# A windowed attention rewritten as banded blocks on small TensorE tiles

## The reference

```python
# x normalised over its last axis; cond = ctx_4096; B = 32, C = 64, T = 512, 8 heads of 8 channels
q = Wq x + bq;  k = Wk cond + bk;  v = Wv cond + bv          # 64 x 64 weights over the 64 rows
k, v = pad by 8 on the left and 7 on the right along T
idx = arange(T)[:, None] + arange(16)[None, :]
dots = einsum('bhdt,bhdtw->bhtw', qh, k[:, :, idx]) * 8 ** -0.5
out = einsum('bhtw,bhdtw->bhdt', softmax(dots), v[:, :, idx])
x = x + tanh(g_xattn[0]) * (Wo out + bo)
```

## Time and profile before

| | |
|---|---|
| median of 3 runs | 1720.14 us (1711.69 to 1721.57) |
| the profiled execution, its own time | 1712.46 us |
| its span | 1710.6 us |
| TensorE / VectorE / GpSimd / ScalarE busy | 80% / 62% / 25% / 25% |
| instructions | 16,681 |
| the first attention in the span | 0 to 637 us |

### The profile page before, as it was taken

The page is one execution under the profiler, slowest core; times in us unless marked ns, Lnnn a source line. Parts: engine busy times, 40 slices in busy tenths (PEclk is TensorE's granted clock), DMA queues, the critical chain, the costliest instruction groups (busy, mean ns, idle before and its releaser), DMA issues. The chain is left out here.

```text
span 1710.6 us, 16681 instructions
## 1 busy us (share of the span) xinstructions
PE 1363.9 (80%) x4738; PEld 798.8 (47%) x4739; DVE 1059.5 (62%) x1664; ACT 421.5 (25%) x1173; POOL 435.7 (25%) x118
## 2 busy tenths in 40 slices
PE   4176578755058639899989998999899979899998
PEld 1032256422047516455545554555455534477753
DVE  3399999999999988235722672257325755522226
ACT  3011210000010023233422442244224422044430
POOL 1366189966069500000000000000000000033225
PEclk9588879978578869999999999999999999899999
DMA  6811140040000035110001000100000017155657
GB/s 221 240 51 72 62 98 0 0 147 0 0 0 0 0 119 202 51 25 1 1 0 25 0 0 0 25 0 0 0 0 0 0 74 319 55 161 166 169 167 253
DMA packets 61266, 115.83 MB, mean 68 GB/s; under 512 B 21280, under 2 KB 25760, under 8 KB 60320
## 3 DMA queue, kind: packets, MB, share of 16 engines
q1 hardware_dynamic: 49296, 82.23, 14.4%
q0 software_dynamic: 6400, 20.98, 4.6%
q10 hardware_dynamic: 5520, 12.06, 1.9%
HBM read 77.50 MB, written 37.75 MB: 67 GB/s over the span
## 5 line engine op out<-in xcount | busy, mean ns | idle before, releaser
L954 POOL DMA_INDIRECT w_sb<-xn_rows,tok_of x48 | 45.6, 949 | 1006.7 <-DVE tok_of L1308 913.7
L242 POOL TENSOR_TENSOR gprod<-dots,v_h 128x4096 f32<-128x4096 f32 x16 | 188.7, 11830 | 115.2 <-ACT dots L282 115.2
L233 POOL TENSOR_TENSOR gprod<-q_h,k_h 128x4096 f32<-128x4096 f32 x16 | 161.9, 10138 | 106.6 <-DMA k_h<-by_row 62.1
L699 PE MATMUL big_ps<-wo_sb,ot 128*128 128x512 f32 x384 | 176.2, 594 | 7.6 <-DVE ot L813 7.6
L318 PE MATMUL sum_ps<-gprod,ident 128*128 128x512 f32 x256 | 122.9, 637 | 70.8 <-POOL gprod L233 50.5
L690 PE MATMUL big_ps<-ht,wq_sb 128*128 128x512 f32 x384 | 171.4, 592 | 0.0
L332 PE MATMUL sum_ps<-gprod,ident 128*128 128x256 f32 x512 | 134.0, 427 | 40.1 <-POOL gprod L242 40.1
L656 ACT ACTIVATE probs<-s_ps,npeak 128x128 f32<-128x128 f32 x256 | 91.8, 363 | 269.8 <-PE p_ps L746 233.0
L332 PEld LDWEIGHTS sum_ps<-gprod,ident 128*128 128x128 f32 x512 | 110.3, 218 | 63.1 <-issue 43.3
L318 PEld LDWEIGHTS sum_ps<-gprod,ident 128*128 128x128 f32 x256 | 51.9, 206 | 141.6 <-issue 85.8
L398 DVE TENSOR_REDUCE o_h<-prod 128x256 f32<-128x4096 f32 x16 | 116.4, 7273 | 0.6
(11 more groups left out here) (193 smaller groups left out, 2170.0 us busy)
## 6 DMA issues: line engine op xcount, KB each, us to landing
wr<-in_w_routed SPq DMA_DIRECT2D x4, 3072.0 KB, 22.4
y_rows<-h_sb SPq DMA_DIRECT2D x48, 256.0 KB, 2.0
by_row<-stage ACTq DMA_DIRECT2D x8, 768.0 KB, 3.8
X<-in_x SPq DMA_DIRECT2D x4, 1024.0 KB, 9.0
cond<-in_ctx SPq DMA_DIRECT2D x16, 256.0 KB, 2.7
by_row<-stage ACTq DMA_DIRECT2D x8, 512.0 KB, 3.3
q_h<-by_row SPq DMA_DIRECT2D x4, 1024.0 KB, 8.6
k_h<-by_row SPq DMA_DIRECT2D x4, 1024.0 KB, 13.2
```

The source lines that it names most:

```text
L233: nc.gpsimd.tensor_tensor(gprod[:, s], q_h[:, :, :], k_h[:, :, bass.ds(4 * i + (2 * s + 1), DIM)], ALU.mult).then_inc(multiplied, 1)
L242: nc.gpsimd.tensor_tensor(by_window(gprod[:, s]), half_of(dots, half), window(d, half), ALU.mult).then_inc(multiplied, 1)
L699: last = nc.tensor.matmul(ps[:, :], ot[:, a % 2, c, k * P:(k + 1) * P], wo_sb[:, a * HC + c, :], start=(c == 0), stop=(c == HC - 1))
```

## The change

The first attention stays in the layout of rows (128 partitions are two batches of 8 heads of 8 channels) and on chip; `by_row` goes. A tile of 128 rows has four quarters of 32 partitions, each four heads (`HG`) of one batch. Positions are cut into blocks of 32 (`BLK`), and a block of queries meets a span of 47 keys (`SPAN`). Scores are dense 32 x 47 blocks; a table `band` adds -1e30 outside the window.

- GpSimd spreads the keys, and likewise the queries, into a block-diagonal form with one copy per head, zero elsewhere (`heads_apart`, L220): 128 x 4 x 512.
- Scores are computed twice. A "score" unit has queries on partitions; VectorE takes its maximum and subtracts it, ScalarE takes the exponential, VectorE sums (L509, L510, L501). Maximum and reciprocal sum (`stats`) are turned by TensorE into rows (L440). A "rescore" unit, one tile later, has the other layout, subtracts the maximum by 16 small matmuls (L401) and goes through ScalarE's exponential into `probs` (`weigh`). A unit covers a quarter and half the positions; there are 8 of each kind per tile, each in one PSUM bank out of six.
- Values: four zero products open the accumulation (L413), then four phases of 64 products on 32x32 tiles (L427), each phase waiting for the one before it. VectorE scales (L527), TensorE applies Wo (L445), ScalarE applies gate and bias, GpSimd adds to X (L231).
- All loops are unrolled in the program. VectorE's first statistics cover four tiles only before the work begins (`deviate`).

The diff, cut to its core (line numbers above are the new kernel's, from L111 on):

```diff
-        q_h = sb("q_h", [P, HD, DIM])
-        k_h = sb("k_h", [P, HD, TPAD])
...
+        q_bd, k_bd = sb("q_bd", [P, 2, HG, SPREAD]), sb("k_bd", [P, 2, HG, SPREAD])
+        v_bd = sb("v_bd", [P, 3, CH, 4, HG, BLK])
...
+        def units(i):
+            order = []
+            for half in range(2):
+                for sc in range(2):
+                    for g in range(2):
+                        first, second = (True, 0, g, sc), (False, 1, g, sc)
+                        if half:
+                            first, second = (False, 0, g, sc), (True, 1, g, sc)
+                        order += [u for u in (first, second) if (i < TILES if u[0] else i > 0)]
+            return order
...
+            def heads_apart(out, a):
+                return nc.gpsimd.tensor_tensor(out, a.unsqueeze(1).to_broadcast([P, HG, DIM]),
+                                               table["head"].unsqueeze(2).to_broadcast([P, HG, DIM]), ALU.mult)
...
+            for i in range(TILES + 1):
+                order = units(i)
...
+                for step in range(len(order) + 3):
+                    for r in range(4):
+                        if step < len(order):
...
+                            nc.tensor.matmul(ps[r * BLK:(r + 1) * BLK, 0:UNIT], ident[rows, rows], band[rows, :],
+                                             start=True, stop=False)
+                        for half in range(2):
+                            if 0 <= step - half - 1 < len(order):
...
+                                if u[0]:
+                                    last = nc.tensor.matmul(dst, q_sb[rows, i % 2, t:t + BLK], k_bd[rows, i % 2, :, t:t + SPAN],
+                                                            start=False, stop=bool(half))
...
+                                    nc.tensor.matmul(dst, k_sb[rows, (i - 1) % 3, t:t + BLK],
+                                                     q_bd[rows, (i - 1) % 2, :, t:t + SPAN], start=False, stop=False)
+                        if 0 <= step - 3 < len(order) and not order[step - 3][0]:
...
+                            for j in range(4):
...
+                                last = nc.tensor.matmul(dst, pick_peak[rows, r, :], window(stats_t[rows, (i - 1) % 2, t:], 2),
+                                                        start=False, stop=(r == 3))
...
+                    for phase in range(4):
+                        if phase:
+                            pe.wait_ge(phase_done, 4 * n + phase)
+                        for c in range(CH):
+                            for h in range(HG):
+                                for j in range(4):
+                                    q = (j + phase) % 4
...
+                                    last = nc.tensor.matmul(out_ps[q * BLK:(q + 1) * BLK, lo:hi], v_bd[rows, n % 3, c, q, h, :],
+                                                            probs[rows, slot(q // 2, q % 2, c // 2), at:at + hi - lo],
+                                                            start=False,
+                                                            stop=(phase == 3 and c == 3 and h == 3))
+                        last.then_inc(phase_done, 1)
...
+                        own.done(V.tensor_reduce(peak[:, e, :], scores, AX_X, ALU.max))
+                        V.tensor_tensor(soft[:, k, :].rearrange("p (a s) -> p a s", s=SPAN), scores,
+                                        peak[:, e, :].unsqueeze(2).to_broadcast([P, 8, SPAN]), ALU.subtract).then_inc(shifted, 1)
```

More of the change, by code:

```diff
@@ L32 @@
 LEFT = WINDOW // 2
-GROUPS = 2
-PAIRS = TILES // GROUPS
-TPAD = DIM + WINDOW
-UNIT = 8
+HG, BLK = HEADS // 2, P // 4
+SPAN = BLK + WINDOW - 1
+UNIT = 2 * HG * SPAN
+SPREAD = DIM + WINDOW
+BANKS = 6
+TABLE_PARTS = (("band", UNIT), ("values_bias", DIM), ("pick_peak", HG * BLK), ("pick_scale", P), ("head", HG),
+               ("zero", 1))
+TABLES = sum(n for _, n in TABLE_PARTS)
 LORA_E, RANK = 8, 16
@@ new lines, in slot @@
+        def slot(b, g, sc):
+            return (b * 2 + g) * 2 + sc
+        bank_of, freed_by = {}, {}
+        history = []
+        for i in range(TILES + 2):
+            items = [("score" if u[0] else "rescore", i, u) for u in units(i)] if i <= TILES else []
+            if i == 0:
+                items = [(kind, n, None) for n in range(2) for kind in ("q", "k", "v")] + items
+            if i + 2 < TILES:
+                items += [(kind, i + 2, None) for kind in ("q", "k", "v")]
+            if i < TILES:
+                items += [("stats", i, None)]
+            if 0 < i <= TILES:
+                items += [("proj", i - 1, None)]
+            history += items
@@ L344, in _ @@
-            for n in range(TILES):
-                if n >= 2:
-                    pe.wait_ge(proj_ready, n - 1)
-                pe.wait_ge(back_in[n % PAIRS], 16 * (n // PAIRS + 1))
-                nc.tensor.matmul(qkv_ps[n % 2][1][:, :], w_sb[:, 3, :], back[n % PAIRS], start=True, stop=True)\
-                  .then_inc(wo_done, 1)
+            freed = {"score": shifted, "rescore": weighed, "q": q_here, "k": k_here, "v": v_here, "stats": stats_here,
+                     "proj": proj_here}
@@ L407, in _, with deviate @@
[L407 to L412 removed]
+            V = nc.vector
+            def deviate(part):
+                tiles = slice(0, 4) if part == 0 else slice(4, TILES)
+                for t in range(tiles.start, tiles.stop):
+                    if t % 4 == 0:
+                        dve.wait_ge(x_in[t // 4], 16)
+                    own.mark(V.bn_stats(bn[:, t, :], X[:, t, :]))
+                own.wait()
+                for t in range(tiles.start, tiles.stop):
+                    own.mark(V.bn_aggr(mv[:, t, :], bn[:, t, :]))
+                own.wait()
+                V.tensor_scalar_add(rstd[:, tiles], mv[:, tiles, 1], EPS).then_inc(var_ready, 1)
+                dve.wait_ge(std_ready, part + 1)
+                own.done(V.reciprocal(rstd[:, tiles], rstd[:, tiles]))
@@ L1419, in laid_out @@
     o["b_qkvo"] = np.stack([np.tile(a[f"L0_xattn_b{k}"], 2) for k in "qkvo"], axis=1)
+    within, key, query = np.arange(P) % BLK, np.arange(SPAN), np.arange(P)
+    ahead = key[None] - within[:, None]
+    band = np.where((ahead >= 0) & (ahead < WINDOW), 0.0, -1e30)
+    pick_peak, pick_scale = np.zeros((P, HG, BLK)), np.zeros((P, P))
+    for h in range(HG):
+        pick_peak[within == h, h, :] = -1.0
+    for block in range(4):
+        for h in range(HG):
+            pick_scale[block * BLK + HG + h, block * BLK + h * HD:block * BLK + (h + 1) * HD] = 1.0
+    tables = {"band": np.tile(band, (1, UNIT // SPAN)), "values_bias": np.tile(a["L0_xattn_bv"], (P, DIM // TOK)),
+              "pick_peak": pick_peak.reshape(P, -1), "pick_scale": pick_scale,
+              "zero": np.zeros((P, 1)), "head": (within[:, None] // HD == np.arange(HG)[None])}
+    o["l0_tables"] = np.concatenate([tables[k].astype(np.float32) for k, _ in TABLE_PARTS], axis=1)
     o["ident_in"] = np.eye(P, dtype=np.float32)
```

514 lines of the change are left out of this document (277 added, 237 removed).

## The result

| | before | after |
|---|---|---|
| median, us | 1718.96 (1711.69 to 1721.57, 4 runs) | 1738.22 (1732.55 to 1748.70, 4 runs) |
| ratio, 95% interval | | 1.0126 (1.0068 to 1.0184) |
| first attention, us of the profiled execution | 637 | 660 |
| the rest, us | 1073.6 | 1075.4 |

The change made the kernel slower by 1.3%. The forecast was 1525 us, faster by 11%: its sign was wrong. The profiled execution after took 1737.27 us for a span of 1735.4.

The account below looks back on a forecast made before the run. VectorE and GpSimd passes were taken to fill the 637 us first attention. Head, iteration 0 (19), fifteen tiles of 25.8 (387), iteration 16 (22) and end (5) gave 450: 1712.5 - 637 + 450 = 1525 us; own range 1460 to 1690, wide 1440 to 2100.

Parts of the forecast that it names:

- I take the low side: tiles overlap, and each step lasts as long as its longest tile: TensorE's score and value phases: 32x32 tiles work side by side, a score step taking 0.628 us; 25.8 us per tile.
- the break-even of 38: First attention: about 38 us for each of 15 full iterations would equal the old stage of 637 us.
- Values: Four value phases per tile on TensorE: 4 x (16 x 0.079 + 0.25 for the wait) = 6.0 us.
- Scores with the wait behind them: Score phase per tile 12.5 us, TensorE and VectorE about even, plus 0.7 us waiting for the last exponential.
- Full-width work: Scale, projections, transposes and output projection per tile: 4.7 us, plus 1.0 of stall for the statistics.
- The stage: New first attention: 450 us, from head, iteration 0, fifteen iterations of 25.8 us, iteration 16 and the end.
- Rival 1: TensorE weight loads go one after another at 31 ns: 42.5 us per tile, 1794 us in all; chance 0.11.
- Rival 2: An f32 matmul's two records block TensorE's queue: 62 us of columns per tile, 2208 us in all; chance 0.16.
- Rival 3: TensorE is granted 1.2 GHz under 32-row tiles: about 23 us more per tile, 1893 us; chance 0.06.
- Rival 4: No overlap at all between TensorE's tiles: 124 + 6.5 us per tile, past 3100 us; chance 0.03.
- The floor of about 25 ns from start to start: TensorE matmul starts: 1160 small records need about 29 us per tile, roughly 1680 us in all.
- The signs named as showing the forecast wrong: Tile time set by a wait on VectorE or GpSimd's spreads, moving the sum by 5 us a tile, or 80 us.

Follow-up runs that it names:

- run 2: Changed kernel with value phases 1 and 2 replaced by phase 0, run three times as a hardware loop: 1631.43 us, against 1746.51 us for the same unrolled.
- runs 10 and 12: 10: changed kernel with bf16 band, merged peak products, peaks' spread in two pieces, 1641.22 us; 12: the same plus values in bf16, 1509.87 us.
- runs 4 and 6: Against the changed kernel: 4, band in one product on a 32x128 tile, 2097.4 us; 6, an added 8-column product on such a tile per score unit, 2109.28 us.

## Why the prediction was wrong

- **The step that failed** is "I take the low side: tiles overlap, and each step lasts as long as its longest tile", not for its overlap but because the sum had no term for bringing the instructions. The text counted "nearly 19,000 matmul records and as many loads in place of 1024 each" and priced them on the array and in the load path only. At 3.6 us per 256 they are 33 us per tile (run 2 takes 512 of them away and gains 7.1); with the full-width part that overlaps little with it, 39, past the break-even of 38 that the prediction had worked out. The page of before had the instruction queue with 19 packets; nothing in the prediction asked what it would become without loops.
- **The rest of the steps** held where the supply was relieved. Values: forecast 6.0 us, 6.35 looped in the tile shown and 7.5 on average. Scores with the wait behind them: forecast 13.2, 11.5 to 12 in runs 10 and 12 (with one pass instead of two for the band and merged peaks, so only roughly the same work). Zero products 0.9 and 0.9. VectorE's passes of 376: forecast 0.55 us, measured 0.547 and 0.549. GpSimd's spread: forecast 5.1 us by half of the earlier trace rows, measured 3.6. The wait for the last exponential 0.7, measured 0.87.
- **Full-width work**: 4.7 + 1.0 forecast, 7.2 measured. Looped, at clock 1.00, it took 4.95, so the excess was the clock. Granted were 0.77 in the value phase and 0.70 behind it, after TensorE had waited for instructions; 0.86 over the whole stage.
- **The stage** came out at 660 us against 450: 584.4 - 387 = 197 in the 15 full tiles, 4 in the head (scores began at 21.3, not 17), -1 in iteration 0 (17.8, not 19) and 9 to 10 in the last iteration and the end (36.5, not 22 + 5). The rest stayed, as forecast. 8 of the 197 are something else than supply: in the first full iteration VectorE, from 38.0 to 46.9 us, works off the statistics of the 12 tiles that were left for later before it takes the first maximum, and the score phase lasts 25.2 us. The forecast counted the gain of that delay in the head and not its price.
- **Rival 1** (loads one after another, 1794 us) came nearest in time and was still not the cause: with all loads in place the looped run took 1631 us. **Rival 2** (the queue blocked by two records to one tile, 2208 us) needed 62 us of columns per tile one after another; the whole tile took 39. **Rival 3** (clock at 1.2 GHz): not under this stream, 0.86; in runs 4 and 6, yes. **Rival 4** falls with rival 2. The floor of about 25 ns from start to start, which the prediction cited from the Trainium skill ("TensorE: Matmul & The Clock Gate", "Wait — 56ns, not 53.3ns?"), is not there between tiles: 512 records in 6.35 us are 12.4 ns each.
- The wide range, 1440 to 2100 us, holds the 1738 measured, but only by way of rivals whose mechanisms did not occur; that is luck. The forecast's own range, 1460 to 1690, does not hold it.
- The signs named as showing the forecast wrong were waits on VectorE or GpSimd. The one that came was a wait on "issue", which the list did not have.

The weight of 0.60 on faster was high for a stream with eighteen times as many matmul records in the same stage, of which the trace of before showed nothing alike.

## What to carry to other kernels

Count what a rewrite sends to one engine as code that must be fetched: unrolled instructions, four for each f32 product on TensorE, by 256 times 3.6 us here. If that nears the stage's time, smaller tiles gain nothing; loop what repeats, merge small products into wide ones, and use bf16 where its precision serves, before touching columns. Then look at the waits again: one of 2 us per tile was worth 23 us here. A busy share of 8 tenths, waits on "issue" at equal counts of records inside an unrolled run (128 matmuls and their loads), and evenly spaced packets in the instruction queue, are how the profile shows it.

## What was not expected of the hardware

- TensorE's instructions arrived at one block of 16 KB per 3.5 to 3.6 us, 14 ns an instruction, while 1024 of them, three quarters from a loop, ran in 6.35 us, 6.2 ns each.
- After a wait on issue the next block's packet started 1.1 us after TensorE had entered the block it waited for, and that block's instructions ran 2.4 us later; around a tile's full-width work no packet started for 9 us.
- Value products on 32x32 tiles started 12.4 ns apart in the loop, each with 39 ns of columns to stream.
- One product of 8 columns on a 32x128 tile among 32x32 ones cost 1.35 us per unit, 346 us in all, and the granted clock fell to 0.55 in the score phase. At full clock the change of tiling alone cost about 0.6 us per unit; how the rest divides stays open.
